# Two-hop context attention: score and value products as three float32r products of high and low parts

## The reference, cut to what matters

```python
def _L1_xattn_ref(context, mem0, W0, W1, mask):      # context = ctx_1024, mem0 = layernorm(x)
    m = (mask == 0)[:, None, :]
    u = mem0
    for W in (W0, W1):
        key_ = jnp.einsum('bpd,md->bpm', u, W)
        attn = jnp.einsum('bpm,blm->bpl', key_, context)      # the score product
        attn = jnp.where(m, neg_inf, attn)
        w = jax.nn.softmax(attn, axis=-1)
        o = jnp.einsum('bpl,bld->bpd', w, context)            # the value product
        u = u + o
    return u
x = x + _L1_xattn_ref(ctx_1024, _layernorm(x, axis=-1), L1_xattn_W0, L1_xattn_W1, mask_BxS2_if1)
```

## Time and profile before

| | |
|---|---|
| timed executions | 1688.71, 1690.71, 1691.66 us; median 1690.71 |
| span of the profiled execution, first to last instruction | 1686.7 us |
| its own device time | not listed apart; the median of the timed runs is 4.0 us above its span |
| busy: TensorE, VectorE, ScalarE, GpSimd | 1589.9, 1030.1, 903.3, 430.4 us |
| `l1_xattn`: first query product to the end of the last value product | 370.2 to 516.6 us |
| TensorE busy between 370 and 518 us | 146.1 of 148 us |

### The profile page before, as it was taken

The page is one execution under the profiler, slowest core; times in us unless marked ns, Lnnn a source line. Parts: engine busy times, 40 slices in busy tenths (PEclk is TensorE's granted clock), DMA queues, the critical chain, the costliest instruction groups (busy, mean ns, idle before and its releaser), DMA issues.

```text
span 1686.7 us, 22273 instructions
## 1 busy us (share of the span) xinstructions
PE 1589.9 (94%) x7467; PEld 814.0 (48%) x7467; DVE 1030.1 (61%) x2136; ACT 903.3 (54%) x1744; POOL 430.4 (26%) x545
## 2 busy tenths in 40 slices
PE   8999998999999899999997999999998999999998
PEld 3344454446666344444334555555343444555446
DVE  7622135573325699999748888888358526555515
ACT  5331324343335587877656778888334745555613
POOL 0000100000000355555304566565120102333300
PEclk9999999999999999999998999999998999999999
DMA  6000100110000000000055321010146110000000
GB/s 241 1 0 0 44 1 1 38 74 1 0 1 20 7 13 10 20 10 26 5 182 191 105 61 30 29 44 16 63 115 195 37 75 30 12 23 12 1 0 25
DMA packets 37159, 74.11 MB, mean 44 GB/s; under 512 B 4475, under 2 KB 23419, under 8 KB 35611
## 3 DMA queue, kind: packets, MB, share of 16 engines
q1 hardware_dynamic: 37046, 72.68, 13.4%
HBM read 55.79 MB, written 16.78 MB: 43 GB/s over the span
## 4 chain that ended last, share of the span: by engine, by line
PE 63%; DVE 7%; ACT 4%; issue 4%; SPq 1%; DMA 1%; POOL 1%; PEldq 0%; PEld 0%; DVEq 0%; POOLq 0%; ACTq 0%
PE ps L2289 6%; PE ps L1873 3%; PE ps L1401 3%; PE ps L1420 3%; PE ps L3208 3%; PE ps L1849 3%; PE ps L1895 3%; PE ps L2278 3%; PE ps L3173 3%; PE ps L3183 3%; PE ps L3228 2%; PE ps L2300 2%; PE ps L1859 2%; PE ps L3201 2%; PE ps L3241 2%
## 5 line engine op out<-in xcount | busy, mean ns | idle before, releaser
L2544 POOL TENSOR_TENSOR work<-work,arena_b 128x512 f32<-128x512 f32 x128 | 168.0, 1315 | 116.4 <-ACT work L2408 116.4
L2498 DVE CUSTOM_DVE_ANT_0 work<-ps,arena_a 128x1024 f32<-128x1024 f32 x128 | 154.6, 1209 | 0.7 <-PE ps L2278 0.7
L2390 ACT ACTIVATE work<-work,small 128x1024 f32<-128x1024 f32 x128 | 146.7, 1146 | 4.7 <-DVE small L2498 4.6
L2289 PE MATMUL ps<-identity,work 128*128 128x128 f32 x1024 | 139.0, 277 | 6.0 <-ACT work L2408 1.8
L2289 PEld LDWEIGHTS ps<-identity,work 128*128 128x128 f32 x1024 | 115.0, 142 | 54.6 <-issue 29.4
L3390 POOL TENSOR_SCALAR ctx_keys<-ctx_keys,small 128x128 f32<-128x128 f32 (+3 forms) x128 | 67.2, 539 | 172.9 <-DVE small L3315 172.9
L2510 DVE TENSOR_TENSOR work<-ps,arena_b 128x512 f32<-128x512 f32 x128 | 87.8, 686 | 32.8 <-PE ps L2289 30.8
L2408 ACT ACTIVATE work<-ps 128x512 f32<-128x512 f32 x128 | 76.3, 596 | 57.6 <-PE ps L2289 54.8
L2065 POOL TENSOR_SCALAR work<-work 128x1024 f32<-128x1024 int32 x64 | 66.7, 1042 | 100.6 <-DVE work L2020 100.1
L2278 PE MATMUL ps<-work 96*128 96x512 bf16 x256 | 79.3, 393 | 13.9 <-DVE small L2498 7.8
L349 PE MATMUL ps<-work,arena_a 128*128 128x512 f32 x192 | 84.6, 593 | 1.8 <-DVE work L246 1.4
(11 more groups left out here) (411 smaller groups left out, 3255.3 us busy)
## 6 DMA issues: line engine op xcount, KB each, us to landing
work<-parts_k_L_xattn SPq DMA_DIRECT2D x14, 384.0 KB, 4.1
arena_a<-in_mask SPq DMA_DIRECT2D x2, 2048.0 KB, 7.7
arena_b<-in_groupT SPq DMA_DIRECT2D x2, 2048.0 KB, 9.4
head_weights<-in_w_L_xattn SPq DMA_DIRECT2D x8, 449.0 KB, 3.2
arena_a<-in_w_l_attn SPq DMA_DIRECT2D x1, 3072.0 KB, 15.3
head_weights<-in_w_L_attn SPq DMA_DIRECT2D x8, 384.0 KB, 3.1
work<-parts_q_L_attn SPq DMA_DIRECT2D x8, 384.0 KB, 4.4
work<-parts_k_L_attn SPq DMA_DIRECT2D x8, 384.0 KB, 4.9
```

Of the source, the lines that this page charges most:

```text
L2289: mm = pe.transpose(t_psum[z][:, kt * P:(kt + 1) * P], prob[i % NP][:, o:o + P], k.iden[:, :])
L2390: act.activation(p, p, ACT.Exp, scale=-1.0, bias=minmax[:, i % 8:i % 8 + 1], accum_out=sums[:, i % 8:i % 8 + 1]).then_inc(*exped.up())
L2498: dve.tensor_tensor_reduce(prob[i % NP], s_psum[i % NS], NEG[:, b, qt, :], -1.0, BIG * 3e8, OP.add, OP.min, minmax[:, i % 8:i % 8 + 1]).th ...
L2544: pool.tensor_tensor(p, p, GT[:, b, 4:8, qt * P:(qt + 1) * P], OP.mult).then_inc(*weighed_pool.up())
```

## The change

Scores and values are no longer one float32 product each, but three float32r products: high x high, high x low, low x high. A high part is a number rounded to float32r, the low part is what is left of it.

- Context: VectorE makes the high parts (`split_high`: tensor_scalar, 128x1024, 8 in all), GpSimd the low parts (`split_low`: tensor_tensor, 128x1024, 8 in all), in place over ctx_feat and ctx_keys. Those of batch 0's ctx_feat are made in `l1_attn`, the others in `l1_xattn`: four high parts behind the mask, two behind L1503 of unit 0.
- Queries: ScalarE's copy rounds to `key_high`; VectorE subtracts it from PSUM (`key_low`, signal `key_rest`), once a batch and hop.
- Probabilities: ScalarE's copies round to `PT_high`; VectorE subtracts each half from `t_psum` (`PT_low`, signal `turned_rest`), twice a unit. `turn_over` of the next unit now waits for `turned_rest`.
- TensorE: 12 matmuls of 512 columns a unit for scores instead of 4, 24 of 256 columns for values instead of 8.
- ctx_feat is loaded again from HBM, one half behind the last score of each batch, and `Values.product` waits for it.

```diff
--- before.py
+++ after.py
@@ -112,7 +112,10 @@
+        self.address = {}
         def sb(name, cols, dt=F32):
+            self.address[name] = -(-nc.sbuf_base // 32) * 32
@@ -142,6 +145,10 @@
+    def rounded(self, name, over, off, cols):
+        return self.nc.alloc_sbuf_tensor_at(name, [P, cols], F32R, offset=self.address[over] + 4 * off)
@@ -1091,6 +1098,7 @@
     now = k.ahead["l1_mix"]
+    parts = ContextParts(k)
@@ -1268,6 +1276,8 @@
             dve.tensor_scalar(wb[:, c, :], ones, k.col("L1_attn_time_decay", c), None, OP.mult).then_inc(*setup.up())
+        for c in range(DC):
+            parts.split_high(dve, parts.feat(0, c))
@@ -1288,11 +1298,57 @@
+    def gpsimd(pool):
+        for c in range(DC):
+            parts.split_low(pool, parts.feat(0, c), c + 1)
...
+    gpsimd(k.pool)
+class ContextParts:
+    def __init__(self, k):
+        self.k = k
+        self.high, self.low = k.signals("dve", 1)[0], k.signals("pool", 1)[0]
+        self.back = k.signals("dma", B)
+        self.feat_high = [view(k.rounded("ctx_feat_high_0", "arena_b", 5120, DC * S2), 0, DC, S2)]
+        self.feat_low = view(k.rounded("ctx_feat_low", "ctx_feat", 0, DC * B * S2), 0, DC, B * S2)
+        k.ahead["ctx_parts"] = self
+    def place(self):
+        k = self.k
+        self.feat_high.append(view(k.rounded("ctx_feat_high_1", "work", 0, DC * S2), 0, DC, S2))
+        self.key_high = view(k.rounded("ctx_keys_high", "work", 2048, 16 * D), 0, 16, D)
+        self.key_low = view(k.rounded("ctx_keys_low", "ctx_keys", 0, 16 * D), 0, 16, D)
+    def feat(self, b, c):
+        o = slice(b * S2, (b + 1) * S2)
+        return self.k.ctxT[:, c, o], self.feat_high[b][:, c, :], self.feat_low[:, c, o]
+    def keys(self, b, j):
+        o = slice(8 * b + 4 * j, 8 * b + 4 * j + 4)
+        return self.k.ctxK[:, o], self.key_high[:, o], self.key_low[:, o]
+    def split_high(self, dve, part):
+        src, high, _ = part
+        dve.tensor_scalar(high, src, 1.0, None, OP.mult).then_inc(*self.high.up())
+    def split_low(self, pool, part, n):
+        src, high, low = part
+        pool.wait_ge(*self.high(n))
+        pool.tensor_tensor(low, src, high.bitcast(F32), OP.subtract).then_inc(*self.low.up())
+    def reload(self, sp, b):
+        src = self.k.a["ctxT"].rearrange("(c p) t -> p c t", p=P)
+        o = slice(b * S2, (b + 1) * S2)
+        sp.dma_start(self.k.ctxT[:, :, o], src[:, :, o]).then_inc(*self.back[b].up())
@@ -1336,10 +1392,14 @@
     u = k.Hn
-    key = view(w, 5 * K, 2, NT)
-    prob = [view(w, (7 + j) * K, S2) for j in range(3)]
-    PT = [view(w, (10 + j) * K, 8, P) for j in range(2)]
-    out = [view(w, 12 * K + j * D, D) for j in range(2)]
+    parts = k.ahead["ctx_parts"]
+    parts.place()
+    key_high = view(k.rounded("queries_high", "work", 6 * K, DC * NT), 0, DC, NT)
+    key_low = view(k.rounded("queries_low", "work", 8 * K, DC * NT), 0, DC, NT)
+    PT_high, PT_low = ([view(k.rounded(f"turned_{n}_{j}", "work", (o + j) * K, S2), 0, 8, P) for j in range(2)]
+                       for n, o in (("high", 10), ("low", 12)))
+    prob = [view(w, (14 + j) * K, S2) for j in range(3)]
+    out = [view(w, 17 * K + j * D, D) for j in range(2)]
@@ -1357,7 +1417,7 @@
     key_out, exped, turned, put = k.signals("act", 4)
-    masked, maxed, recip, added, resid = k.signals("dve", 5)
+    masked, maxed, recip, added, resid, key_rest, turned_rest = k.signals("dve", 7)
@@ -1365,6 +1425,9 @@
         Values(k).load(sp)
+        for b in range(B):
+            sp.wait_ge(*scored(4 * (B + b) + 4))
+            parts.reload(sp, b)
@@ -1396,10 +1459,20 @@
                     pe.wait_ge(*maxed(i - 1 if qt else i))
+                if hop == 0 and qt == 0:
+                    pe.wait_ge(*parts.low(6 if b else 2))
...
                     for c in range(DC):
-                        mm = pe.matmul(ps[:, half(hf)], key[:, c, q0:q0 + P],
-                                       k.ctxT[:, c, b * S2 + hf * S:b * S2 + (hf + 1) * S], start=c == 0, stop=c == 1)
+                        pe.matmul(ps[:, half(hf)], key_high[:, c, q0:q0 + P], parts.feat_high[b][:, c, half(hf)],
+                                  start=c == 0, stop=False)
+                        o = b * S2 + hf * S
+                        pe.matmul(ps[:, half(hf)], key_high[:, c, q0:q0 + P], parts.feat_low[:, c, o:o + S],
+                                  start=False, stop=False)
+                pe.wait_ge(*key_rest(i // 4 + 1))
+                for hf in range(2):
+                    for c in range(DC):
+                        mm = pe.matmul(ps[:, half(hf)], key_low[:, c, q0:q0 + P], parts.feat_high[b][:, c, half(hf)],
+                                       start=False, stop=c == 1)
@@ -1413,11 +1486,19 @@
             if 0 <= i < N:
+                b = units[i][1]
                 pe.wait_ge(*turned(2 * i + 2))
+                if i in (0, 4):
+                    pe.wait_ge(*parts.low(8 if b else 4))
...
                 for kt in range(8):
-                    mm = pe.matmul(o_psum, PT[i % 2][:, kt, :], k.ctxK[:, units[i][1] * 8 + kt, :], start=kt == 0,
+                    pe.matmul(o_psum, PT_high[i % 2][:, kt, :], parts.key_high[:, b * 8 + kt, :], start=kt == 0,
+                              stop=False)
+                    pe.matmul(o_psum, PT_high[i % 2][:, kt, :], parts.key_low[:, b * 8 + kt, :], start=False, stop=False)
+                pe.wait_ge(*turned_rest(2 * i + 2))
+                for kt in range(8):
+                    mm = pe.matmul(o_psum, PT_low[i % 2][:, kt, :], parts.key_high[:, b * 8 + kt, :], start=False,
                                    stop=kt == 7)
@@ -1430,7 +1511,7 @@
             if i:
-                pe.wait_ge(*turned(2 * i - 1 + hf))
+                pe.wait_ge(*turned_rest(2 * i - 1 + hf))
@@ -1444,7 +1525,7 @@
                     act.wait_ge(*keyed(i // 4 + 1))
-                    act.activation(key[:, :, half(b)], s_psum[key_slot(i // 4)].rearrange("p (c s) -> p c s", c=2),
+                    act.activation(key_high[:, :, half(b)], s_psum[key_slot(i // 4)].rearrange("p (c s) -> p c s", c=2),
                                    ACT.Copy).then_inc(*key_out.up())
@@ -1457,7 +1538,7 @@
                         act.wait_ge(*pv(i - 1))
-                    act.activation(PT[i % 2][:, 4 * hf:4 * hf + 4, :].rearrange("p k t -> p (k t)"), t_psum[hf],
+                    act.activation(PT_high[i % 2][:, 4 * hf:4 * hf + 4, :].rearrange("p k t -> p (k t)"), t_psum[hf],
                                    ACT.Copy).then_inc(*turned.up())
@@ -1476,6 +1557,10 @@
         dve.tensor_scalar(madd, mraw, 0.0, FMIN, OP.is_equal, OP.mult).then_inc(*masked.up())
+        for j in range(2):
+            parts.split_high(dve, parts.keys(0, j))
+        for c in range(DC):
+            parts.split_high(dve, parts.feat(1, c))
@@ -1490,6 +1575,11 @@
                 nm, su, rs = cols(i)
+                if i % 4 == 0:
+                    j = i // 4
+                    dve.wait_ge(*key_out(j + 1))
+                    dve.tensor_tensor(key_low[:, :, half(b)], s_psum[key_slot(j)].rearrange("p (c s) -> p c s", c=2),
+                                      key_high[:, :, half(b)].bitcast(F32), OP.subtract).then_inc(*key_rest.up())
@@ -1501,6 +1591,16 @@
                 dve.reciprocal(rs, su).then_inc(*recip.up())
+                if i == 0:
+                    for j in range(2):
+                        parts.split_high(dve, parts.keys(1, j))
+            i = step - 1
+            if 0 <= i < N:
+                for hf in range(2):
+                    dve.wait_ge(*turned(2 * i + hf + 1))
+                    dve.tensor_tensor(PT_low[i % 2][:, 4 * hf:4 * hf + 4, :].rearrange("p k t -> p (k t)"), t_psum[hf],
+                                      PT_high[i % 2][:, 4 * hf:4 * hf + 4, :].rearrange("p k t -> p (k t)").bitcast(F32),
+                                      OP.subtract).then_inc(*turned_rest.up())
@@ -1521,6 +1621,12 @@
     def gpsimd(pool):
+        for j in range(2):
+            parts.split_low(pool, parts.keys(0, j), 3 + j)
+        for c in range(DC):
+            parts.split_low(pool, parts.feat(1, c), 5 + c)
+        for j in range(2):
+            parts.split_low(pool, parts.keys(1, j), 7 + j)
@@ -2111,6 +2217,8 @@
             pe.wait_ge(*self.loaded(1))
+        if j % 4 == 0:
+            pe.wait_ge(*self.k.ahead["ctx_parts"].back[j // 4](1))
@@ -3549,6 +3657,7 @@
                 if cols:
+                    k.address["work"] = -(-nc.sbuf_base // 32) * 32
```

## The result

The changed kernel takes 1677.65 us in the median (four runs, 1676.67 to 1678.68), beside 1691.18 us for the kernel before in the same comparison (1688.71 to 1692.52). The ratio is 0.9926, with a 95% interval from 0.9914 to 0.9938: 13.5 us faster, where 1679.3 was forecast. The span of the profiled execution went from 1686.7 to 1675.3 us.

What follows compares the result with a forecast made beforehand. The prediction took TensorE's stream to bound this stage. A gross 20.6 us less waits of 3.5, 1.75, 3.6 and 0.3 gave 11.4 us, so 1690.7 would become 1679.3 us; range 1670 to 1688.

Steps and rivals of the forecast that it cites:

- The gross gain: TensorE's saving over 16 units, 0.71 us each on scores and 0.58 on values: 20.6 us before waits.
- The rival of weights that are not hidden: Values: float32r weight loads do not run behind short matmuls, 0.187 us a matmul; about 1700 us, chance 0.10.
- V: Pace of a 256-column float32r value matmul with its own 128x128 weights, taken as 0.120 us.
- the other reading (0.113): Value matmul's pace in us if the 0.013 excess scaled with columns instead of being fixed per matmul.
- Start and unit 1, 3.5 + 1.75: TensorE waits 3.5 us for `key_low` at the stage's start, then 1.75 us at `turn_over(1)`, behind VectorE's high parts.
- the *Clock* rival: TensorE's idle waits lower its clock, two or three stretches costing 3.4 to 5 us; chance 0.14, shared with longer waits.
- one of the prediction's own signs of being wrong: The prediction is wrong if the clock falls in this stage for more than 5 us.
- Steps 4 and 8, 1.8 each: Quantization of 5.9 us stands ahead of `key_low` on VectorE, so TensorE waits 1.8 us at each.
- T: The end of a unit's scores, from which the prediction counts when each engine is ready.
- End, 0.3: No scores lie between the last two turnings, so the second half of `turn_over(15)` waits 0.3 us.
- The sum: Gross 20.6 us less waits of 3.5, 1.75, 3.6 and 0.3: 11.4 us faster.
- Hidden work: Plain-unit subtractions, ScalarE's copies, parts made in `l1_attn` and the reloads were put at no cost.

Runs made afterwards that it cites:

- The first experiment: Against the changed kernel, GpSimd's first subtraction in the stage waits for `key_low` of batch 0; 1678.93 us, ratio 0.9938.
- The second experiment: Against the changed kernel, 16 bf16 matmuls with unread results stand ahead of TensorE's wait for `key_low` in unit 0; 1678.39 us, ratio 0.993.
- the third experiment: Against the changed kernel, batch 1's four high parts go one by one to the end of steps 0 to 3; 1682.55 us, ratio 0.9956.

## Why the prediction was right, step by step

**The gross gain.** Scores were put at 12 x 0.227 = 2.72; the pace is 0.232 and they take 2.79, a gain of 0.64 instead of 0.71. Values were put at 24 x 0.120 = 2.88, a gain of 0.58; the pace is 0.117 to 0.118, and the unit's 1.26 leaves them 0.62. The two errors nearly cancel: 16 x 1.26 = 20.2 against 20.6. The rival of weights that are not hidden is refuted by 0.118. The choice of 0.120 for V was in part luck. It took the excess over half a float32 pass as 0.013 for every matmul, and here the excess is 0.018 at 512 columns (0.232 - 0.214) and 0.011 at 256 (0.118 - 0.107): it shrinks with the matmul, as in the other reading (0.113), and was saved by a pace of 512 columns that is higher here than in `l3_ffn`. The Trainium skill's formula ("TensorE: Matmul & The Clock Gate", back-to-back issue gap) gives 109 ns, and the trace does not follow it.

**Start and unit 1, 3.5 + 1.75.** The first term came out, 3.49, for the reason given: the third and the fourth high part take 2.87 and 2.84 us. The first experiment shows it, since the wait ends with GpSimd's silence. The second shows as 0.26, because the *Clock* rival set in between: the granted clock was at the lower level from 380.4 to 387.2. Up to unit 3 the stage had lost 6.9 us of its gross gain (the length up to the end of unit 1's scores grew by 5.06 although two units of scores gave 1.28; the two units behind it gained 0.5 less than they should). Of these, 3.49 and 0.26 are waits; the rest, 3.1, is the lower clock and refilling. The second experiment puts a price on it: without the lower clock the wait for `turned_low` is 1.24, near the forecast 1.75, and the net gain 1.5. So the step that failed is that the forecast let this rival stand aside, at 1.7 us for a stretch, and took the full wait instead: 5.25 against 6.9. The stretch was 6.8 us long, not the 3.4 behind the idle of the earlier trace rows, so that one of the prediction's own signs of being wrong came true (the clock falls in this stage for more than 5 us). The time came near the forecast all the same because other terms were too large.

The row that the rival rested on does not decide whether a stretch comes, either. In the kernel after the same four passes stand behind the same idle, and the clock stays at 1.00:

```profile
1367.49 1.98 PE L3031 MATMUL ps<-arena_a 128*128 128x512 f32 x4 [2.08 <-DVE arena_a L3149]
```

Before, they took 2.87 us.

**Steps 4 and 8, 1.8 each.** The place and the cause were right, and the size too large: 0.93 and 0.87 of wait, 1.20 and 1.14 us with the refilling. VectorE was reckoned to be ready at T + 12.1 (4.9 + 5.9 + 1.2 is 12.0) and was at T + 11.7, in part since its instructions start before the one ahead is quite over (407.94 + 1.23 is 409.17, yet the next starts at 409.08). TensorE was reckoned there at T + 10.3 and came at T + 10.6 to 10.8. That the waits are 1.81 and 1.71 when TensorE has less to do, the size forecast, is a coincidence.

**End, 0.3.** `turn_over(15)` takes 1.15 us instead of 0.87: 0.28.

**The sum.** 20.2 - 6.9 - 2.3 - 0.3 = 10.7, and the stage became 10.6 shorter; the forecast was 20.6 - 9.15 = 11.4. Too small a term at the start and too large ones at units 4 and 8 make up for each other: 9.5 against 9.15. That is luck, and not the working. The median went down by 13.5, 2 us more than forecast; this lies within what single executions differ by, and was not traced further.

**Hidden work.** The subtractions of plain units and ScalarE's copies cost nothing, as argued, and the parts made in `l1_attn` next to nothing: the first scan starts 0.63 us later than before (321.79), of which 0.6 was there ahead of them. The reloads landed in 5.5 us, the second about 499, and their first reader starts at 512.07.

**What the forecast did not see.** GpSimd needs 5.55 to 5.73 us between its last subtraction and the first reduction. In the kernel after 13.68 us of idle time cover it, so it did not touch the result; in the third experiment that cover was 0 and it cost the whole gain of the edit.

## What to carry to other kernels

Each part of this change alone took its full gain (10.6 and 9.3 us), and both together only 10.6: preparing work, put in a block ahead of an instruction that the full engine waits for, ate the rest, with the lower clock that followed the longest wait. Spread such work one piece per unit, behind the instruction that is waited for, and move away the old work that stands in front of it (here the quantization) too; one of the two alone changed the stage by -2.4 or even +3.1 us, both by -8.3. Where the first GpSimd reduction follows GpSimd arithmetic, keep some 6 us between them.

## What the hardware showed

GpSimd's change from tensor arithmetic to the program's first PARTITION_ALL_REDUCE took 5.73 and 5.55 us in the two runs that do not hide it, started after the last arithmetic, and appears as "issue" behind two MODIFY_POOL_CONFIG records.

Not every VectorE instruction is held beside GpSimd's subtractions. Two TENSOR_SCALAR with one input, from SBUF to SBUF, took 3.88 or 5.62 us instead of 1.28, and two TENSOR_TENSOR with both inputs in SBUF 3.33 instead of 1.29. A TENSOR_TENSOR with one input in PSUM and one in SBUF was not: `queries_low` took 1.21 us at 380.25 in the kernel after, and 1.21 at 376.73 with GpSimd silent. The Trainium skill ("GPSIMD Engine Reference", 1. Specifications) names two SBUF inputs and two-port modes as the cases of contention. The rows agree for two SBUF inputs, 3.33 us instead of 1.29; that the one-input form runs in a two-port mode, no row shows.

In this stage the clock fell around every wait of 3.48 us or more: 3.49 in the kernel after and with the quantization spread, 3.48 with low products left out, then 3.85, 5.44 and 8.02. It did not after those of up to 1.81. In between, one idle of the program gave both: 2.07 us with the lower level behind it before the change, and 2.08 us without it after.
